# Differential attention in a list schedule: scores in halves and single PSUM banks, stacks in five transfers

## The chip, the cores and the metric

One core of one Trainium2 chip. The metric is the device time of one execution in microseconds, median of the runs; lower is better.

## What is computed

Four layers in a row, each followed by an addition and a layer normalisation of `x`, 4 x 1024 tokens of width 256: a linear attention (stage a), a gated network (stage b), a differential attention (stage c) and two blocks of local attention with a gated network (stage d). The change is in stage c:

```python
q = rope_rotate((x @ Wq.T).reshape(b, s, 2 * H, D)).reshape(b, s, H, 2, D)    # H = 8, D = 16
k = rope_rotate((x @ Wk.T).reshape(b, s, 2 * H, D)).reshape(b, s, H, 2, D)
v = (x @ Wv.T)                                          # 8 heads of 32
o1 = softmax(q1 k1^T * D ** -0.25) v
o2 = softmax(q2 k2^T * D ** -0.25) v
o = o1 - lam * o2
o = (o * rsqrt(mean(o ** 2) + EPS) * ln_w + ln_b) * (1 - LAMBDA_INIT)
return o @ Wo.T
```

There are 4 batches of 1024 tokens and 16 half heads, so 64 attention maps of 1024 x 1024.

## The kernel before

Every engine's program is written by a plan. `Plan.add` appends a step with the count of increments each engine makes in it; `play` then lets each engine emit its part of every step in the plan's order. Each engine works through its queue strictly in that order. PSUM is eight banks of 512 columns, `ps0` to `ps3` and the halves of `pw0` and `pw1`; a `Ring` hands out banks and keeps, for each, the step that frees it.

Stage c works on one map after the other, (n, sh) in the order `maps`, four maps to a group n, sixteen to a batch, in eight steps kt of 128 keys. In a step TensorE makes

- the scores of 128 keys with all 1024 queries, in two matmuls of 512 columns (lines 1327 to 1340, `half_of_s`). Their 50 rows hold q and k split into a high and a low part, and two rows with the maxima;
- beside each of them, in the other half of the array's rows, a `c_max` (line 1315), the scores of a map two places ahead (`LEAD` is 32 halves), only for their row maxima. The two are called a pair below;
- the weighting `c_w` (line 1351): exponentials times values, in two column halves at once, summed over the eight steps in one bank (the accumulator, `c_pv`).

ScalarE makes the exponential of a step's scores in one instruction of 1024 columns (line 1637) into one of two `c_p`. VectorE takes the maximum of each `c_max` (line 1922). After a map's last `c_max`, `c_mm` joins the maxima, `c_row` transposes them (TensorE, ScalarE, VectorE) and two transfers put them into `c_qst`. After a map's last weighting, ScalarE copies the accumulator out (`c_o`, line 1644), TensorE transposes it (`c_ft`, four 128x128 through line 1131) and VectorE divides. Once for four maps the normalisation follows (`c_n1` on ScalarE, `c_n2` and `c_n3` on VectorE and POOL), and per batch eight projections: `c_ot` transposes two blocks, `c_wo` multiplies (line 206).

Before a batch can start, `c_x` transposes the rows of x, `c_val` makes the values, `c_rot` the rotated q and k, `c_sum` and `c_part` on POOL split them, and `c_stack` (line 2377) copies them over SP's queue into the rows of `c_qst` and `c_kst`, once per map, in six transfers of 64 KB.

The order of stage c is written by hand in `plan_c`. `weigh()` emits the scores of step k + 1, then the weighting of step k. `finish_head`, `normalise`, `project`, `values`, `rotated` are generators that are advanced by one piece at fixed places between them. Scores take double banks (`wide`, two of them), maxima two single banks, and two banks are left: one is the accumulator, the other serves everything else in turn. Other stages use `Order`, a list scheduler: each operation has a due time, a modelled duration (`TOOK`), what it comes after, what banks it takes and gives, and the scheduler places the operation with the earliest due time among those that could start within `eps` of the first.

Of the kernel before, what the change touches and what calls it, by code (L numbers as in the profile page):

```python
# [209 lines left out]
def build(nc, A, out):  # L210
    with ExitStack() as ctx:
# [25 lines left out]
        with ExitStack() as c3:  # L237
# [295 lines left out]
        def plan_c():  # L533
            P.land("tabs", 2, "c_tabs")
            P.add("c_tabs")
            bank, sbank, wide = Ring(range(8)), Ring([]), Ring([])
# [55 lines left out]
            def weigh():
                order = [(n, sh, kt) for n, sh in maps for kt in range(8)]

                def scores(n, sh, kt):
                    P.take(wide, "c_s", n, sh, kt)
                    P.add("c_s0", n, sh, kt)
                    next(ahead, None)
                    P.add("c_s", n, sh, kt, pe=1, act=1)
                    wide.give(slot["c_s", (n, sh, kt)], ("act", "c_s", n, sh, kt))  # L600
                    if next(ahead, "end") == "end":
                        count[0] += 16

                scores(*order[0])
                for k, (n, sh, kt) in enumerate(order):
                    if k + 1 < len(order):
                        scores(*order[k + 1])
                    yield 0
                    if kt == 0:
                        slot["c_pv", (n, sh)], room["c_pv", (n, sh)] = pvb[0]  # L610
                    P.add("c_w", n, sh, kt, pe=1)
                    while late and late[0][-1] <= count[0]:
                        rows()
                    if kt == 7:
                        if n + 2 < 16:
                            held.append((n + 2, sh))
                        P.add("c_o", n, sh, act=1)
                        pvb[0] = bank.idle.pop(0)
                        bank.give(slot["c_pv", (n, sh)], ("act", "c_o", n, sh))
                        post.append(finish_head(n, sh))  # L620
                    if kt in (3, 7) and held and held[0][0] // 4 in turned_by:
                        stack(*held.pop(0))
                    yield 1

            def finish_head(n, sh):
                yield
                yield
                b, s16 = n // 4, 4 * (n % 4) + sh
                if s16 % 2:
                    P.take(bank, "c_ft", n, sh)  # L630
                    P.take(tmps, "c_odd", n, sh)
                    P.add("c_ft", n, sh, pe=1, dve=3, pool=1)
                    tmps.give(slot["c_odd", (n, sh)], ("pool", "c_ft", n, sh))
                    bank.give(slot["c_ft", (n, sh)], ("dve", "c_ft", n, sh))
                else:
                    P.use(bank, "dve", "c_ft", n, sh, pe=1, dve=2)
                if s16 % 4 == 3 and (b, s16) != (3, 15):
# [1917 lines left out]
```

## Time and profile before

| | us |
|---|---|
| median of 3 runs | 2985.62 (2983.31 to 2985.84) |
| the profiled execution | 2988.65, its span 2986.5 |
| TensorE busy in the span | 2847.9 (95%) |
| VectorE, ScalarE, POOL busy | 2170.7 (73%), 1611.5 (54%), 1049.8 (35%) |
| stage c, first score to the last c_ft | 522.7 to 1582.8 |

In the rows below, PE is TensorE, PEld its loading of weights, DVE VectorE, ACT ScalarE, SPq the queue of transfers. A timeline's row has the start, the length, the engine, the line, the operation with what it writes and reads, how many instructions are merged, and in brackets how long the engine had been idle and what ended that. A matmul's end is modelled and the next one may start before it, so costs are best read from start to start. A matmul of 32-bit values stands in two instructions, so a weighting has four.

### The profile page before, as it was taken

To read this page: it belongs to the slowest core of one execution; us is meant where nothing else is said; L and a number is where in the kernel's file an instruction comes from. 1 tells how busy PE (TensorE), PEld (TensorE's weight loads), DVE (VectorE), ACT (ScalarE), POOL (GpSimd) and SP (SyncE) were. 2 spreads that over 40 slices of the span, in tenths; PEclk is the share of its full clock that TensorE was granted. 3 is DMA by queue.
4 is the path that set the end of the run, shared out by engine and by line. 5 is a ranking of instruction groups with operands and counts; after the bars stand their busy time and mean duration, and the time that the engine had idled before them with its cause. 6 is when DMAs were issued, how large, how long until landed. Compare 5 with 4: busy or idle time off the path is not lost.

```text
span 2986.5 us, 52437 instructions
## 1 busy us (share of the span) xinstructions
PE 2847.9 (95%) x20384; PEld 1928.0 (65%) x20384; DVE 2170.7 (73%) x5057; ACT 1611.5 (54%) x2976; POOL 1049.8 (35%) x1210
## 2 busy tenths in 40 slices
PE   8998999999999999999997899999999899999997
PEld 7777877333333333333335788888888788888886
DVE  7885445777787778787865677777777577788784
ACT  3222332465555555465664566666676566666662
POOL 4333432014112211412233343444454444444441
PEclk9999999999999999999998899999999999999998
DMA  2000010220321122032202000000010100000001
GB/s 77 23 9 22 8 22 3 34 32 6 43 23 17 22 33 24 10 40 26 47 12 87 13 5 5 5 4 4 12 32 15 28 27 4 12 11 12 12 11 58
DMA packets 46795, 66.63 MB, mean 22 GB/s; under 512 B 10174, under 2 KB 34772, under 8 KB 46548
## 3 DMA queue, kind: packets, MB, share of 16 engines
q1 hardware_dynamic: 46548, 63.29, 12.0%
q8 instruction: 161, 2.64, 0.4%
q14 instruction: 86, 0.70, 0.1%
HBM read 24.99 MB, written 8.39 MB: 11 GB/s over the span
## 4 chain that ended last, share of the span: by engine, by line
PE 74%; DVE 12%; DMA 5%; ACT 3%; POOL 3%; issue 1%; SPq 1%; POOLq 0%; ACTq 0%; DVEq 0%
PE ps L1351 17%; PE pw L206 12%; PE ps L206 11%; PE pw L1327 9%; PE ps L1131 4%; DMA e_hs<-x 4%; PE pw L1131 4%; PE ps L1511 4%; PE pw L1424 2%; PE pw L1462 2%; PE pw L1281 1%; PE pw L1444 1%; PE ps L1315 1%; DVE c_mx L1922 1%; DVE stat L1791 1%
## 5 line engine op out<-in xcount | busy, mean ns | idle before, releaser
L1637 ACT ACTIVATE c_p<-pw 128x1024 f32<-128x1024 f32 x512 | 522.6, 1021 | 429.8 <-PE ps L1315 348.3
L1922 DVE TENSOR_REDUCE c_mx<-ps 128x1 f32<-128x512 f32 x1024 | 658.5, 683 | 124.4 <-PE ps L1315 120.9
L1351 PE MATMUL ps<-c_p,c_v 128*64 128x512 f32 x2048 | 555.8, 620 | 8.2 <-DVE c_mr L1935 7.7
L1315 PE MATMUL ps<-c_kst,c_qst 48*128 48x512 f32 x1024 | 386.4, 451 | 6.7 <-DMA c_kst<-shared 3.4
L1327 PE MATMUL pw<-c_qst,c_kst 50*128 50x512 f32 x1024 | 376.9, 447 | 0.8 <-DVE c_v L1895 0.8
L1327 PEld LDWEIGHTS pw<-c_qst,c_kst 50*128 50x128 f32 x1024 | 152.5, 185 | 314.9 <-issue 302.6
L1690 ACT ACTIVATE e_sm<-e_sm,e_mx 128x256 f32<-128x256 f32 x512 | 253.9, 498 | 62.6 <-DVE e_mx L2066 62.4
L2186 POOL TENSOR_SCALAR stat<-stat 128x1 f32<-128x1 f32 (+1 forms) x138 | 32.1, 233 | 669.8 <-DVE stat L1794 401.6
L206 PE MATMUL pw<-shared,e_xb 128*128 128x512 f32 x792 | 217.6, 413 | 2.3 <-DVE e_xb L2015 1.6
L2290 POOL TENSOR_TENSOR e_ss<-e_ss,half 128x16 f32<-128x16 f32 x64 | 186.7, 2918 | 87.2 <-DVE e_ss L2023 66.4
L1351 PEld LDWEIGHTS ps<-c_p,c_v 128*64 128x64 f32 x2048 | 103.0, 135 | 166.0 <-issue 128.7
L1315 PEld LDWEIGHTS ps<-c_kst,c_qst 48*128 48x128 f32 x1024 | 169.9, 185 | 28.2 <-DVE c_mx L1922 12.3
L2250 POOL TENSOR_TENSOR c_o<-c_o,c_t 128x128 f32<-128x128 f32 x32 | 14.8, 464 | 478.7 <-DVE c_t L1968 465.1
L206 PE MATMUL pw<-shared,e_w 128*124 128x512 f32 (+1 forms) x672 | 176.7, 403 | 0.4 <-ACT e_pt L1698 0.2
L1511 PE MATMUL ps<-e_w,e_hp 124*128 124x256 f32 (+1 forms) x1152 | 162.9, 291 | 8.7 <-POOL e_hp L2311 7.1
L2066 DVE CUSTOM_DVE_ANT_0 e_sm<-pw,e_mask,e_ss 128x256 f32<-128x256 f32 x354 | 152.0, 476 | 24.6 <-PE pw L1424 15.9
L1791 DVE BATCH_NORM_STATS2 stat<-x 128x6 f32<-128x256 f32 (+1 forms) x192 | 67.5, 374 | 129.6 <-DMA e_hs<-x 129.1
L206 PEld LDWEIGHTS pw<-shared,e_xb 128*128 128x128 f32 x792 | 142.2, 192 | 30.0 <-DVE e_xb L2015 1.8
L1511 PEld LDWEIGHTS ps<-e_w,e_hp 124*128 124x128 f32 (+1 forms) x1152 | 146.1, 194 | 14.6 <-POOL e_hp L2311 8.1
L206 PEld LDWEIGHTS pw<-shared,e_w 128*124 128x124 f32 (+1 forms) x672 | 120.3, 186 | 29.8 <-ACT e_of L1707 1.4
L1424 PE MATMUL pw<-e_k,e_qt 64*128 64x128 f32 x1416 | 133.1, 282 | 1.8 <-ACT e_pt L1698 0.9
L1131 PE MATMUL pw<-ident,e_sm 128*128 128x128 f32 x680 | 103.7, 280 | 22.6 <-ACT e_sm L1690 20.4
(309 smaller groups left out, 6154.7 us busy)
## 6 DMA issues: line engine op xcount, KB each, us to landing
c_qst<-shared SPq DMA_DIRECT2D x192, 64.0 KB
c_kst<-shared SPq DMA_DIRECT2D x192, 64.0 KB
x<-in_L_attn_x SPq DMA_DIRECT2D x8, 512.0 KB, 3.9
keep<-x SPq DMA_DIRECT2D x8, 512.0 KB, 4.5
e_raw<-keep SPq DMA_DIRECT2D x8, 512.0 KB, 3.5
out<-x SPq DMA_DIRECT2D x8, 512.0 KB, 5.9
e_hs<-x SPq DMA_DIRECT2D x64, 63.5 KB
e_raw<-in_L_ffn_w SPq DMA_DIRECT2D x10, 248.0 KB
```

Source lines behind the costliest of these rows:

```text
L206: ins = e.matmul(o, l, r, start=first and n == 1, stop=n == 3 * len(parts), skip_group_check=True)
L1131: ins = e.transpose(o, v, ident[0:v.shape[0], 0:v.shape[0]])
L1315: e.matmul(bank_of("c_max", n, sh, qt, h), c_qst[i][p0:p0 + 48, sh // 2, 128 * qt:128 * qt + 128], c_kst[i][p0:p0 + 48, sh // 2, 512 * h:5 ...
L1327: return e.matmul(p[:, 512 * h:512 * h + 512], c_kst[i][p0:p0 + 50, sh // 2, 128 * kt:128 * kt + 128], c_qst[i][p0:p0 + 50, sh // 2, 512 * ...
L1351: ins = e.matmul(pv[64 * h:64 * h + 64, :], c_v[b % 2][:, kt, 33 * hd:33 * hd + 64], p[:, 512 * h:512 * h + 512], start=kt == 0, stop=kt = ...
L1424: ins = e.matmul(p[r][:, c0:c0 + 128], qt[rs, hb, :], kk[rs, hb, :], start=True, stop=True, skip_group_check=True)
L1511: ins = e.matmul(o, hp[kk, l_, 128 * i:128 * i + 128], d_w2[kk, r, j, :], start=j == 0 and i % 2 == 0 and n == 0, stop=j == 5 and n == 2, ...
L1637: e.activation(c_p[kt % 2][:, :], wides[slot["c_s", (n, sh, kt)]], ACT.Exp, scale=0.5).then_inc(SC, 1)
L1690: e.activation(sm[:, q, :], sm[:, q, :], ACT.Exp, bias=mx[:, 0, q:q + 1], scale=-1.0, accum_out=mx[:, 1, q:q + 1]).then_inc(SC, 1)
L1922: e.tensor_reduce(c_mx[m % 2][:, qt, h:h + 1], bank_of("c_max", n, sh, qt, h), AX.X, ALU.max).then_inc(VE, 1)
L2066: e.tensor_tensor_reduce(d_sm[s][:, q, :], p[:, 256 * h:256 * h + 256], d_mask[:, 1 if win % 8 else 0, :], st[:, 2, head:head + 1], 3.0e38 ...
L2290: e.tensor_tensor(st[:, 1, :], st[:, 0, :], half[:, :], ALU.pow).then_inc(GP, 1)
```

## The change

Stage c is now placed by `Order`. Its operations get durations, due times (`DUE_C`, in a period `PACE` of 16.73 us per map) and their dependences; TensorE's results are held to be there 0.22 us after an operation, a change between pairs and other work to cost 0.09. With it come:

- scores are two separate operations per step, each in a single bank, of which there are three; each half has its own exponential of 512 columns (ACT `c_s`), and there are four `c_p` instead of two;
- the maxima have three banks instead of two; two banks are left for accumulator and everything else, as before, but both come from one ring;
- a stack is five transfers: one of 32 partitions and four of 16, instead of six of 16. The scratch tensor `shared` is laid out so that high and low parts lie together;
- one `c_v` (`c_vals`) instead of two, so a `c_val` waits for the weighting of the batch before that read its place;
- the weights of the next stage, its tables (`d_tabs`, with semaphores of their own) and `d_scl` are placed by the same scheduler.

```diff
+PACE, NEAR = 16.73, 0.16
+DUE_C = {"pe c_s": -2.7, "act c_s": 13.5, "dve c_max": 12.3, "dve c_mm": -8.4, "c_row": -19.7, "row_in": -24.9,
...
-                c_v = [sbin(c, f"c_v{i}", [128, 8, 296]) for i in range(2)]
-                c_p = [sbin(c, f"c_p{i}", [128, S]) for i in range(2)]
+                c_v = sbin(c, "c_vals", [128, 8, 336])
+                c_p = [sbin(c, f"c_p{i}", [128, S]) for i in range(4)]
...
-            wide.idle = [(k, tuple(a for b in (4 + 2 * k, 5 + 2 * k) for a in bank.drop(b)[1])) for k in range(2)]
-            pvb = [bank.drop(2)]
...
+            sbank.idle.append(bank.drop(4))
+            scores.idle = [bank.drop(k) for k in (5, 6, 7)]
             P.add("c_lam", dve=6, act=1)
+            order = Order(P, NEAR, {"pe": 0.22}, 0.06, 0.09)
...
+                op(at(m, "pe c_s", kt + h / 2), "pe", "c_s", i, 1, after + ([("pe", "c_s", *before)] if q else []), takes, place=place,
+                   mode="pair")
+                op(at(m, "act c_s", kt + h / 2), "act", "c_s", i, 1, [("pe", "c_s", *i)] + ([("act", "c_s", *before)] if q else []),
+                   [(weighed, "c_p", *maps[m], kt)] * (1 - h), [(scores, "c_s", *i)])
...
+                op(at(m + 1, "act c_o"), "act", "c_o", i, 1, [("pe", "c_w", *i, 7)] + ([("pe", "c_ft", *maps[m - 1])] if m else []),
+                   gives=[(bank, "c_pv", *i)])
+                op(at(m + 1, "pe c_ft"), "pe", "c_ft", i, 1, [("act", "c_o", *i)], [(bank, "c_ft", *i)])
...
+                        op(at(16 * b, "c_val", kt), "pe", "c_val", i, 1, [("dve", "c_x", b, nb, k) for k in range(2)] +
+                           [("pe", "c_w", *maps[16 * b - 1], kt)], [(bank, "c_val", *i)])
...
-            def c_s(n, sh, kt):
-                b4 = 8 * nth[n, sh] + kt
-                w.wait_ge(*pe("c_w", *maps[(b4 - 2) // 8], (b4 - 2) % 8) if b4 >= 2 else pe("c_s", n, sh, kt))
-                w.wait_ge(*pe("c_s", n, sh, kt))
-                e.activation(c_p[kt % 2][:, :], wides[slot["c_s", (n, sh, kt)]], ACT.Exp, scale=0.5).then_inc(SC, 1)
+            def c_s(n, sh, kt, h):
+                if h == 0:
+                    for s in freed("c_p", n, sh, kt):
+                        w.wait_ge(*s)
+                w.wait_ge(*pe("c_s", n, sh, kt, h))
+                e.activation(c_p[slot["c_p", (n, sh, kt)]][:, 512 * h:512 * h + 512], bank_of("c_s", n, sh, kt, h), ACT.Exp,
+                             scale=0.5).then_inc(SC, 1)
...
-                for dst, qk, order in ((c_qst[i], 0, (0, 0, 1)), (c_kst[i], 1, (0, 1, 0))):
-                    for r, part in enumerate(order):
-                        p = p0 + 16 * r
-                        e.dma_start(raw32(dst[p:p + 16, sh // 2, :]),
-                                    raw32(both[r0:r0 + 8, :, qk, part, :])).then_inc(landed, 16)
+                q, k = [raw32(both[r0:r0 + 8, qk, :, :, :]) for qk in range(2)]
+                low, high = slice(p0, p0 + 32), slice(p0 + 32, p0 + 48)
+                e.dma_start(raw32(c_qst[i][low, sh // 2, :]), q.rearrange("p m b n -> p (m b) n")).then_inc(landed, 16)
+                for b in range(2):
+                    e.dma_start(raw32(c_kst[i][p0 + b:p0 + 32:2, sh // 2, :]), k[:, :, 0, :]).then_inc(landed, 16)
+                e.dma_start(raw32(c_qst[i][high, sh // 2, :]), q[:, :, 0, :]).then_inc(landed, 16)
+                e.dma_start(raw32(c_kst[i][high, sh // 2, :]), k[:, :, 1, :]).then_inc(landed, 16)
```

How the rows move is shown at three places. L1327 before and L1381 now are scores, L1315 and L1364 maxima, L1351 and L1394 weightings, L1131 and L1180 transpositions.

TensorE in a plain map, from the first weighting of a map to the `c_ft` of the one before it; before:

```order
L1351 MATMUL ps3<-c_p0,c_v0 64x512 x2
L1327 MATMUL pw0<-c_qst1,c_kst1 128x512
L1315 MATMUL ps0<-c_kst1,c_qst1 128x512
L1327 MATMUL pw0<-c_qst1,c_kst1 128x512
L1315 MATMUL ps1<-c_kst1,c_qst1 128x512
L1351 MATMUL ps3<-c_p1,c_v0 64x512 x2
L1327 MATMUL pw1<-c_qst1,c_kst1 128x512
L1315 MATMUL ps0<-c_kst1,c_qst1 128x512
L1327 MATMUL pw1<-c_qst1,c_kst1 128x512
L1315 MATMUL ps1<-c_kst1,c_qst1 128x512
L1131 MATMUL ps2<-ident,c_pv 128x128 x4
L1351 MATMUL ps3<-c_p0,c_v0 64x512 x2
```

and now, the row of `c_p3` being the last weighting of the old map:

```order
L1381 MATMUL pw1<-c_qst1,c_kst1 128x512
L1364 MATMUL pw0<-c_kst0,c_qst0 128x512
L1394 MATMUL ps2<-c_p3,c_vals 64x512 x2
L1381 MATMUL pw0<-c_qst1,c_kst1 128x512
L1364 MATMUL ps0<-c_kst0,c_qst0 128x512
L1381 MATMUL pw1<-c_qst1,c_kst1 128x512
L1364 MATMUL ps1<-c_kst0,c_qst0 128x512
L1180 MATMUL ps3<-ident,c_pv 128x128 x4
L1394 MATMUL ps2<-c_p0,c_vals 64x512 x2
```

The `c_ft` (`c_pv`) stood behind two weightings of the new map, in the other bank; now it stands two pairs behind the last weighting of its own map and ahead of the new map's first one, which goes on in `ps2`. The scores now go through single halves. Seen from a weighting, four half scores had been issued beyond those of the steps before it, and now seven.

ScalarE at the same place (`c_pv` is `c_o`), before:

```order
L1637 ACTIVATE c_p0<-pw0 128x1024
L1613 ACTIVATE c_mr2<-ps3 8x128
L1644 ACTIVATE c_pv<-ps2 128x512
L1637 ACTIVATE c_p1<-pw1 128x1024
L1637 ACTIVATE c_p0<-pw0 128x1024
L1637 ACTIVATE c_p1<-pw1 128x1024
```

and now:

```order
L1682 ACTIVATE c_p0<-pw1 128x512
L1682 ACTIVATE c_p1<-pw0 128x512
L1682 ACTIVATE c_p1<-pw1 128x512
L1682 ACTIVATE c_p2<-pw1 128x512
L1690 ACTIVATE c_pv<-ps2 128x512
L1682 ACTIVATE c_p2<-pw0 128x512
L1682 ACTIVATE c_p3<-pw1 128x512 x2
```

What was one exponential is two, and `c_o` stands between the halves of one step.

VectorE at the start of the stage, before:

```order
L1947 TENSOR_SCALAR c_ls<-c_ls 128x1
L1922 TENSOR_REDUCE c_mx0<-ps0 128x1
L1922 TENSOR_REDUCE c_mx0<-ps1 128x1
L1922 TENSOR_REDUCE c_mx0<-ps0 128x1
L1922 TENSOR_REDUCE c_mx0<-ps1 128x1
L1935 TENSOR_TENSOR c_mr1<-ps3,c_mr1 8x128
```

and now:

```order
L1991 TENSOR_REDUCE c_ls<-c_lt 128x2
L1993 TENSOR_SCALAR c_ls<-c_ls 128x1
L1837 BN_STATS stat<-x 128x6 x4
L1840 BN_AGGR stat<-stat 128x2 x4
L1968 TENSOR_REDUCE c_mx0<-ps0 128x1
L1968 TENSOR_REDUCE c_mx0<-ps1 128x1
L1933 TENSOR_TENSOR c_xb0<-ps3,c_xb0 128x512
L1854 TENSOR_SCALAR x<-x,stat 128x256 x4
L1968 TENSOR_REDUCE c_mx0<-pw0 128x1
```

The statistics of the last tile of stage b, which came sixteen maxima later, now stand ahead of the first of them.

## Rows read from the trace of the kernel before

**Rows 1.** Busy times in stage c: length, busy us (instructions) by engine, clock, DMA, GB/s

```profile
522.70:1582.80 1060.10, 1027.68 (x4907) 387.94 (x4907) 800.93 (x1574) 590.00 (x692) 245.39 (x313) 0.99 0.22 26
```

**Rows 2.** Timeline of a plain stretch: start us, busy us, engine, line, what

```profile
1001.28 0.50 PE L1327 MATMUL pw<-c_qst,c_kst 50*128 50x512 f32 x1
...
1001.61 0.39 PE L1327 MATMUL pw<-c_qst,c_kst 50*128 50x512 f32 x1
...
1001.94 1.08 PE L1351 MATMUL ps<-c_p,c_v 128*64 128x512 f32 x4
1002.10 1.02 ACT L1637 ACTIVATE c_p<-pw 128x1024 f32<-128x1024 f32 x1 [0.65 <-PE ps L1315]
...
1002.95 0.50 PE L1327 MATMUL pw<-c_qst,c_kst 50*128 50x512 f32 x1
...
1004.63 0.27 PE L1131 MATMUL ps<-ident,c_mm 128*8 128x128 f32 x1
...
1009.07 0.66 PE L1131 MATMUL ps<-ident,c_pv 128*128 128x128 f32 x4
```

**Rows 3.** Timeline of TensorE, groups of the other kinds (two stretches)

```profile
666.69 1.67 PE L206 MATMUL ps<-c_xb,c_q 128*128 128x512 f32 x6
...
1364.88 0.44 PE L1131 MATMUL ps<-ident,c_o 128*128 128x128 f32 x2
...
1366.92 0.97 PE L206 MATMUL ps<-c_o,c_at 128*128 128x256 f32 x6
```

**Rows 4.** Busy times in five stretches, columns as in rows 1

```profile
522.70:589.68 66.98, 62.89 (x292) 25.16 (x292) 46.80 (x98) 32.70 (x40) 1.27 (x2) 0.92 0.28 32
589.68:661.75 72.07, 71.28 (x347) 24.94 (x345) 57.54 (x110) 44.56 (x51) 9.64 (x13) 1.00 0.31 34
661.75:736.39 74.64, 72.16 (x327) 28.20 (x325) 55.92 (x104) 35.89 (x41) 33.78 (x35) 1.00 0.05 6
779.69:905.67 125.98, 120.87 (x613) 49.38 (x611) 98.21 (x205) 68.54 (x84) 23.24 (x36) 1.00 0.25 28
...
1325.33:1443.28 117.95, 112.55 (x550) 42.82 (x548) 92.71 (x194) 66.01 (x80) 23.96 (x38) 0.99 0.26 28
```

**Rows 5.** Timeline of TensorE around a c_x

```profile
543.44 0.50 PE L1327 MATMUL pw<-c_qst,c_kst 50*128 50x512 f32 x1
544.27 0.49 PE L1315 MATMUL ps<-c_kst,c_qst 48*128 48x512 f32 x1 [0.34 <-DVE c_mx L1922]
...
545.30 1.08 PE L1351 MATMUL ps<-c_p,c_v 128*64 128x512 f32 x4
```

**Rows 6.** Timeline of TensorE, first weighting of a plain map after c_row

```profile
600.75 1.08 PE L1351 MATMUL ps<-c_p,c_v 128*64 128x512 f32 x4 [0.16 <-DVE c_mr L1935]
```

**Rows 7.** Timeline of TensorE at the end of the stage

```profile
1581.04 1.08 PE L1351 MATMUL ps<-c_p,c_v 128*64 128x512 f32 x4 [0.17 <-ACT c_p L1637]
1582.82 0.66 PE L1131 MATMUL ps<-ident,c_pv 128*128 128x128 f32 x4 [0.70 <-ACT c_pv L1644]
```

**Rows 8.** Groups in the stage: xcount, busy us, mean ns, idle before

```profile
L1637 ACT ACTIVATE c_p<-pw 128x1024 f32<-128x1024 f32 x512 | 522.6, 1021 | 429.8 <-PE ps L1315 348.3 <-PE pw L1327 79.0
...
L1644 ACT ACTIVATE c_pv<-ps 128x512 f32<-128x512 f32 x64 | 36.5, 570 | 1.2 <-PE ps L1351 1.2
...
L1791 DVE BATCH_NORM_STATS2 stat<-x 128x6 f32<-128x256 f32 x28 | 11.4, 415 | 0.0
```

**Rows 9.** Timeline from a batch's last c_ft to the first c_ot (two stretches)

```profile
1339.72 0.66 PE L1131 MATMUL ps<-ident,c_pv 128*128 128x128 f32 x4
...
1352.18 0.72 POOL L2274 TENSOR_TENSOR c_o<-c_o,c_lnb 128x256 f32<-128x256 f32 x1
...
1353.15 0.41 PE L1131 MATMUL ps<-ident,c_o 128*128 128x128 f32 x2 [3.11 <-POOL c_o L2274]
```

**Rows 10.** Timeline of TensorE near the start, at the lower clock

```profile
529.69 1.97 PE L1351 MATMUL ps<-c_p,c_v 128*64 128x512 f32 x4
...
532.74 1.97 PE L1351 MATMUL ps<-c_p,c_v 128*64 128x512 f32 x4
```

More of the change, by code:

```diff
@@ L44 @@
        "dve n_nm": 43.9, "d_x": -1.4}
+PACE, NEAR = 16.73, 0.16
+DUE_C = {"pe c_s": -2.7, "act c_s": 13.5, "dve c_max": 12.3, "dve c_mm": -8.4, "c_row": -19.7, "row_in": -24.9,
+         "c_stack": -4.2, "pe c_w": 4.4, "act c_o": 21, "pe c_ft": -11.4, "dve c_ft": -18.8, "pool c_ft": 27.2,
+         "c_n": -28.1, "c_val": -1, "c_x": -1.2, "c_rot": 143.7, "pool c_sum": 129.1, "pool c_part": 132.4,
+         "c_ot": 8, "c_wo": 40.4, "n_c": 19.5}
 PACE_A, NEAR_A = 8.4, 0.06
@@ L535, in plan_c @@
             P.add("c_tabs")
-            bank, sbank, wide = Ring(range(8)), Ring([]), Ring([])
+            bank, sbank, scores, weighed = Ring(range(8)), Ring([]), Ring([]), Ring(range(4))
             tmps, pairs = Ring(range(2)), Ring(range(1))
@@ L588, in rows @@
                 n, sh, _ = late.pop(0)
-                P.land(f"row{n % 2}{sh}", 2, "c_row", n, sh)
                 P.use(bank, "dve", "c_row", n, sh, pe=1, act=1, dve=1)
[L592 to L637, printed above, removed]
-                    post.append(normalise(b, s16 // 4))
-                yield
@@ L772, in plan_c, with at, moved, place @@
-            while post:
-                advance(post)
+            while late:
+                rows()
+            sbank.idle.append(bank.drop(4))
+            scores.idle = [bank.drop(k) for k in (5, 6, 7)]
+            P.add("c_lam", dve=6, act=1)
+            order = Order(P, NEAR, {"pe": 0.22}, 0.06, 0.09)
+            op = order.op
+            def at(m, key, k=0.0):
+                return PACE * (m + k / 8) + DUE_C[key]
+            def moved(due, name, count, kind, i, after):
+                def place(t):
+                    P.land(name, count, kind, *i)
+                    P.add(kind, *i)
+                    order.over_at["dma", kind, i] = t + 2.2
+                    order.settle([("dma", kind, i)])
+                op(due, "sp", kind, i, 1, after, place=place)
@@ new lines, in normalised @@
+            def normalised(b, u):
+                i, m = (b, u), 4 * (4 * b + u) + 4
+                before = [("pool", "c_n3", *divmod(4 * b + u - 2, 4))] if 4 * b + u > 1 else []
+                op(at(m, "c_n"), "act", "c_n1", i, 1, [("pool", "c_ft", 4 * b + u, sh) for sh in (1, 3)], [(tmps, "c_n1", *i)])
+                op(at(m, "c_n"), "dve", "c_n2", i, 1, [("act", "c_n1", *i)] + before, gives=[(tmps, "c_n1", *i)])
+                op(at(m, "c_n"), "pool", "c_n2", i, 2, [("dve", "c_n2", *i)])
+                op(at(m, "c_n"), "pool", "c_n3", i, 5, [("pool", "c_n2", *i)])
@@ new lines, in plan_c @@
+            i = ("b", 7)
+            op(0, "dve", "n_st", i, 8, [("dve", "b_add", 7, 1)])
+            op(0, "pool", "n_st", i, 2, [("dve", "n_st", *i)])
+            op(0, "dve", "n_nm", i, 4, [("pool", "n_st", *i)])
+            for n in range(1, 16):
+                for sh in TURN:
+                    stacked(n, sh)
+            for m in range(64):
+                for kt in range(8):
+                    for h in range(2):
+                        scored(m, kt, h)
+                weighing(m)
+                if m > 1:
+                    row(m)
@@ L774, in plan_c @@
+            for b in range(4):
+                for u in range(4 if b < 3 else 3):
+                    normalised(b, u)
+                for q in range(8 if b < 3 else 0):
+                    projected(b, q)
+                if b:
+                    rows_of(b)
+                    turned_rows(b)
+            next_layer()
+            order.run(1e8)
+            assert not order.blocked and not order.ready, (list(order.blocked)[:9], [(o["eng"], o["kind"], o["i"]) for o in order.ready])
             P.add("d_begin")
```

272 lines of the change are left out of this document (147 added, 125 removed).

## The prediction

> **What bounds the kernel now.** I read the page's busy times, then cut the trace into the stage that the change touches and into stretches of it, then timelines. The order of instructions is the same in both kernels up to the first score of the differential attention and again from the last transposition of its output, on TensorE row by row, so this stage alone is priced. It lasts 1060.1 us, from the first score at 522.70 to that transposition at 1582.80, and TensorE is busy for 1027.7 of them, VectorE for 800.9, ScalarE for 590.0 [rows 1]. So TensorE bounds it, and the question is how much of its time is waiting, open or hidden in the distance between starts.
>
> What a step costs when nothing waits is read from starts. Two score pairs and the weighting after them repeat after 1002.95 - 1001.28 = 1.67 us, of which the pairs take 0.66 and the weighting 1.01 [rows 2]. A weighting's busy time is 1.08, so a group's last matmul runs 0.07 into the next group. Less that, the c_row transposition takes 0.20 and the four of c_ft 0.59 [rows 2], the two of c_ot 0.37, c_wo 0.90, c_rot 1.60 [rows 3]. A map of eight steps is then 8 x 1.67 + 0.20 + 0.59 = 14.15 us. The whole stage: 64 x 14.15 - 0.2 (one c_row of map 1 is made before it) = 905.4, and 12 c_x (0.59), 24 c_val (0.90, the shape of c_wo), 24 c_rot, 24 c_ot, 24 c_wo: 7.1 + 21.6 + 38.4 + 8.9 + 21.6 = 97.6. Sum **1003 us**. The stage spends **57 us** above it. That is all that an order can win.
>
> Where the 57 lie [rows 4]: the first stretch lasts 66.98 against 56.3 by the counts, 10.7 lost; its clock is 0.92. Five plain maps last 72.07 against 70.75: 0.26 each, and about 27 maps are of this kind, 7 us. Four maps with eight c_rot last 74.64 against 56.6 + 12.8 = 69.4: 5.2, and there are three such stretches, 16 us. Seven maps with c_x, c_val, c_ot, c_wo last 125.98 against 118.8: 7.2, a second like it some 7.5, and the third without c_x and c_val 117.95 against 109.2: 8.7; together 23.5. The last step loses 1. Sum 58, within 1 us of the 57.
>
> **The change part by part.** *Banks of the maxima and scores.* Maxima get three banks instead of two, scores three single ones instead of two double ones. Around a c_x of the kernel before, the second maximum waits for VectorE: from 543.44 to 545.30 are 1.86 us for two pairs that need 0.66 [rows 5]. One more bank lets VectorE be later by half a step or more before TensorE stops. VectorE is busy 57.54 of 72.07 us in plain maps and 98.21 of 125.98 in the fullest ones [rows 4], so it can catch up. This is the largest gain, in the 33 maps with extra work. Bounds for what these maps lose now, 39 us: nothing of it goes, or all.
>
> *Place of the accumulator.* Before, a new map's weighting takes the bank that c_row has just used, and waits 0.16 for the DVE c_mr that empties it [rows 6]; this, with what it shifts, is the 0.26 of a plain map. In the new order c_row has its own bank, and the new map goes on in the bank that c_o empties, or in the other.
>
> *The new wait.* Before, c_ft stands behind two weightings of the next map, over 3 us after the last weighting. Now only two pairs lie between: the order gives c_ft 1.01 + 0.66 = 1.67 us. The kernel before has this case once, at its end, with ScalarE idle: the last weighting starts at 1581.04, c_ft at 1582.82, 1.78 us [rows 7]. So at least 0.11 is lost per map, 7 us over 63 maps, if the ACT c_o finds its engine free. It stands behind the exponentials of the pairs before that weighting. An exponential of half the width is not in the trace: 1.021 us for 1024 columns bounds it above, half of it, 0.51, below, and the nearest row is c_o itself, 512 columns at 0.570 [rows 8]; I take 0.59. An exponential starts 0.49 after its pair (1002.10 after 1001.61) [rows 2]. For pairs 0.66 and 0.33 ahead of the weighting that is -0.17 and, behind the first, +0.42, so the second ends 1.01 after the weighting's start, and the weighting's last matmul ends at 1.08 [rows 2]. They just fit. I take 0.11 and keep 0.68 (one exponential more ahead) for the range. What is queued behind c_o on ScalarE are exponentials with 2.5 steps of lead: the weighting now stands seven half scores behind instead of four, with four c_p. Behind c_ft on TensorE stand the new map's first weighting and all the rest.
>
> *ScalarE by halves:* 512 x (2 x 0.59 - 1.02) = 82 us more, 672 of some 1030: hidden under TensorE, and without the seven halves of lead it would cost 0.16 per step at most.
>
> *Stacks, SP and POOL.* Five transfers instead of six carry the same bytes. A stack must be there for maxima two maps ahead of its scores, six maps after the score that frees its place: nothing gained, nothing lost. The row transfers stand behind one stack per map at worst and have a map of slack. On POOL the d_scl and the six weight splits swap places; both are before the last three head groups. Two c_fill fewer: nothing, they run beside c_val. One c_v instead of two ties c_val to the last weightings of the batch before: pairs and a weighting (1.34 us or more) lie between two c_val, against 0.42 us of copy.
>
> *Moved work near POOL.* The first c_ot of a batch follows c_ft of its last map through DVE, POOL and ACT. Before, that took from 1339.72 to 1353.15, 13.4 us, once with 3.1 us of stall [rows 9]. In the new order 5 weightings, 4 c_val and 9 pairs lie between, 0.59 + 5.05 + 3.6 + 2.97 = 12.2: about 1 us lost in each of three batches, 3 us in all. A c_rot pair on one bank with one weighting and one pair between (five times) leaves 1.34 us to two DVE operations of 0.69 and those ahead of them: 0.3 to 1.0 each, 3 us.
>
> *The start.* The eight statistics of the last b tile now stand ahead of the first maxima: four at 0.415 [rows 8] and four shorter ones, 2 to 4 us on VectorE, where the second step waited for a maximum anyway. Three banks give half of it back. I leave the 10.7 at 10, keeping 7 and 14.
>
> **Sum.** Start 10 + plain maps 27 x 0.11 = 3 + c_rot maps 12 x 0.11 + 3 = 4.3 + the 21 fullest maps 21 x 0.11 + 3 for c_ot + 4 for queued VectorE work = 9.3 + end 1 = 27.6 us above 1003, against 57: **29 us less**. The profiled execution took 2988.65 (span 2986.5 and 2.1 around it) and would take 2959; the median of the runs is 3.0 lower, 2985.62, so I predict **2957 us**, 1.0% faster. A measurement of this kernel tells 0.2%, 6 us, from no change.
>
> **The rivals.** *VectorE keeps the full maps* (0.14): its queue, not the banks, is late there, 39 us stay and only the plain maps and part of the rot maps gain: about 11 us, **2975**. For it: VectorE's share rises to 78%, and in-order waits as for c_mr remain. Against: its idle time there is over 20%.
>
> *The clock flickers* (0.05). In the first stretch TensorE waited and then ran at half clock: a weighting and the pairs ahead of the next one took 532.74 - 529.69 = 3.05 us instead of 1.67 [rows 10], at 1.2 and not 2.4 GHz. If the new short stops at every map did this for a twentieth of the stage, 51 us at 3.05 instead of 1.67 lose 23: **2980**. Against it: five plain maps with a stop each have a clock of 1.00 [rows 4]. The Trainium skill (TensorE: Matmul & The Clock Gate, A second HAM failure mode: psum-queue depth-cycling) says that frequent short idles between groups of matmuls, as banks are cycled, can make the clock swing between its levels. By that rule the change is mostly eaten; by the row on plain maps it is not, and I side with the row.
>
> *The order does not do what it says* (0.07): it rests on durations (a step of 1.78 by its table, 1.67 in the trace) and every engine's queue is strict, so new waits appear where the plan sees none, and 57 stay 57 within 6: **2986**.
>
> *c_o comes late: slower* (0.08). If one more exponential is ahead of c_o or halves take 0.7 and more, c_ft starts 0.11 + 0.57 = 0.68 late in each of 63 maps: 43 us in place of 7. Then 27.6 + 36 = 64 against 57: **2993**. It decides from (57 - 20.6) / 63 = 0.58 us per map, where the gain is gone. For it: nothing but two pairs covers c_o, once per map. Against: ScalarE has more than a quarter of its time free.
>
> **How the numbers follow.** Forecast 0.66, from 2944 (20 us more of the full maps' and start's waits gone, less what c_o takes) to 2970. The range goes on to the VectorE case and stops short of the others: **2943 to 2979**, leaving out 0.2. Faster: forecast and VectorE case, 0.80. Same: the order case and part of the clock's, 0.11. Slower 0.09.
>
> **What would show it.** Right: the stage lasts about 1031 us; plain maps take 14.2 to 14.3 from c_ft to c_ft; c_ft's wait for c_pv is 0.1 in each; hardly any maximum waits for VectorE; ACT busy near 670. Wrong: plain maps over 14.4 (c_o late), clock below 0.95 in the middle of the stage, or maxima still waiting in the maps with c_val and c_wo; or a score that waits for a row's transfer.

## The result and the profile after

The changed kernel takes **2959.48 us** (median of 4 runs, 2956.85 to 2962.04) against 2985.73 (4 runs, 2983.31 to 2988.52): a ratio of 0.9912, 95% interval 0.9895 to 0.9929. Forecast were 2957 us, between 2943 and 2979. The profiled execution took 2961.68 us, its span 2959.4.

Busy times by stretch: the stage, the plain maps 4 to 7, the maps 8 to 11 with rotations, maps 16 to 23 and 48 to 55 with c_val and projections, and all that follows the stage. Columns as in [rows 1].

```profile
520.89:1552.20 1031.31, 1014.23 (x4911) 367.15 (x4910) 806.38 (x1575) 632.89 (x1204) 244.58 (x313) 1.00 0.22 27
591.00:648.08 57.08, 56.94 (x278) 17.91 (x277) 46.05 (x88) 38.27 (x74) 8.78 (x11) 1.00 0.27 29
648.08:717.64 69.56, 69.42 (x325) 26.29 (x324) 56.35 (x104) 38.39 (x74) 33.44 (x35) 1.00 0.02 3
780.77:911.75 130.98, 129.82 (x663) 49.35 (x661) 108.43 (x220) 82.98 (x160) 22.41 (x34) 1.00 0.23 25
1312.42:1440.52 128.10, 127.22 (x647) 47.70 (x645) 105.67 (x216) 81.02 (x156) 22.38 (x34) 1.00 0.23 25
1552.20:2957.00 1404.80, 1322.28 (x11107) 1140.72 (x11105) 1035.66 (x2738) 869.32 (x2000) 601.97 (x638) 0.97 0.06 19
```

The stage lasts 1031.3 us instead of 1060.1 [rows 1], 28.8 less; the span shrank by 27.1 (1.8 less ahead of the stage, 3.5 more behind it). A plain map takes 57.08 / 4 = 14.27 us. Four rotation maps take 69.56 against 69.4 by the prediction's counts, where it was 5.2 above them before [rows 4]. Maps 16 to 23 hold eight steps each and five c_val, eight c_ot, seven c_wo, four c_x: 113.2 + 4.5 + 3.0 + 6.3 + 2.3 = 129.3, measured 130.98; before, seven such maps lost 7.2.

The groups that answer to [rows 8], in the stage (count, busy us, mean ns, idle before):

```profile
L1682 ACT ACTIVATE c_p<-pw 128x512 f32<-128x512 f32 x1024 | 562.3, 595 | 341.2 <-PE ps L1364 183.5 <-PE pw L1364 87.8 <-PE pw L1381 46.5
...
L1690 ACT ACTIVATE c_pv<-ps 128x512 f32<-128x512 f32 x64 | 38.2, 598 | 13.7 <-PE ps L1394 13.7
...
L1837 DVE BATCH_NORM_STATS2 stat<-x 128x6 f32<-128x256 f32 x28 | 11.7, 426 | 0.8
```

TensorE around the c_ft that opens map 5 (the last weighting of map 4 starts at 602.90), and the stage's end, which answers to [rows 7]:

```profile
602.90 1.08 PE L1394 MATMUL ps<-c_p,c_vals 128*64 128x512 f32 x4
...
604.68 0.66 PE L1180 MATMUL ps<-ident,c_pv 128*128 128x128 f32 x4
605.26 1.08 PE L1394 MATMUL ps<-c_p,c_vals 128*64 128x512 f32 x4
...
1551.79 0.65 PE L1180 MATMUL ps<-ident,c_pv 128*128 128x128 f32 x4 [0.70 <-ACT c_pv L1690]
```

From weighting to c_ft are 1.78 us where 1.67 is work: the 0.11 of the forecast. The waits of TensorE in the stage show what it did not have:

```profile
PE pw L1381 <- DMA c_qst<-c_mr: 9.0, 8, 2.4
...
PE ps L1394 <- ACT c_p L1682: 1.4, 1, 1.4
```

Eight times a score waits for its map's row (the transfer of c_mr into c_qst), 9.0 us in all. No wait on a maximum stands among the longer ones, and none on POOL before the stage's end. With each map's length from its first weighting to the next map's, less the counts, 28 us above 1003 are left (good to about 1 us a line, as a c_wo that stands at the border of two maps can be given to either):

| maps | above the counts, before | after | forecast |
|---|---|---|---|
| 0 to 3, and what stands ahead | 11.0 | 8.8 | 10 |
| a plain map | 0.26 | 0.11 | 0.11 |
| 12 rotation maps | 16 | 0.4 | 4.3 |
| 26 other maps with c_val or projections | 23.5 | 2.7 | 9.3 |
| 13 to 15, 29 to 31, 45 to 47 | 2.3 | 14.7 | in the plain maps |

The forecast's sum held; two of its terms did not. One that it set at nothing holds about 16 us: 4.2 us in map 1, and most of the last line. Two that it kept, the waits of the maps with extra work and those of the start, are for the most part gone.

### The profile page after: what moved, and what is told of

Same layout as the page of the kernel before. It is cut to its first block, busy times and chain, and to the rows that moved or that the text cites. A ratio compares the mean times of both kernels' runs of the same rounds, so it can differ in the third digit from the quotient of the medians.

```text
span 2959.4 us, 52471 instructions
## 1 busy us (share of the span) xinstructions
PE 2835.6 (96%) x20384; PEld 1908.3 (64%) x20384; DVE 2176.4 (74%) x5057; ACT 1653.3 (56%) x3488; POOL 1048.7 (35%) x1208
## 4 chain that ended last, share of the span: by engine, by line
PE 75%; DVE 11%; DMA 6%; POOL 3%; ACT 2%; issue 1%; SPq 1%; POOLq 0%; DVEq 0%; ACTq 0%
PE ps L1394 17%; PE pw L218 13%; PE ps L218 11%; PE pw L1381 10%; PE ps L1180 5%; DMA e_hs<-x 4%; PE pw L1180 4%; PE ps L1554 4%; PE pw L1467 2%; PE pw L1505 2%; PE pw L1330 1%; PE pw L1487 1%; DVE stat L1837 1%; DVE e_ot L2132 1%; PE ps L1467 1%
## 5 line engine op out<-in xcount | busy, mean ns | idle before, releaser
L1682 ACT ACTIVATE c_p<-pw 128x512 f32<-128x512 f32 x1024 | 562.3, 595 | 341.2 <-PE ps L1364 183.5
L1394 PE MATMUL ps<-c_p,c_vals 128*64 128x512 f32 x2048 | 547.4, 618 | 2.7 <-ACT c_p L1682 1.4
L1968 DVE TENSOR_REDUCE c_mx<-ps 128x1 f32<-128x512 f32 x694 | 462.7, 683 | 114.3 <-PE ps L1364 106.7
L1381 PE MATMUL pw<-c_qst,c_kst 50*128 50x512 f32 x1024 | 385.1, 449 | 9.4 <-DMA c_qst<-c_mr 9.0
L1381 PEld LDWEIGHTS pw<-c_qst,c_kst 50*128 50x128 f32 x1024 | 154.5, 185 | 368.2 <-ACT c_p L1682 272.1
L1364 PE MATMUL ps<-c_kst,c_qst 48*128 48x512 f32 x694 | 289.5, 452 | 4.6 <-DMA c_kst<-shared 3.5
L1968 DVE TENSOR_REDUCE c_mx<-pw 128x1 f32<-128x512 f32 x330 | 225.5, 683 | 47.3 <-PE pw L1364 43.8
L1394 PEld LDWEIGHTS ps<-c_p,c_vals 128*64 128x64 f32 x2048 | 104.2, 135 | 181.2 <-issue 162.1
L1364 PE MATMUL pw<-c_kst,c_qst 48*128 48x512 f32 x330 | 148.2, 449 | 0.0
```

The costliest lines, as they stand in the source:

```text
L1364: e.matmul(bank_of("c_max", n, sh, qt, h), c_qst[i][p0:p0 + 48, sh // 2, 128 * qt:128 * qt + 128], c_kst[i][p0:p0 + 48, sh // 2, 512 * h:5 ...
L1381: e.matmul(bank_of("c_s", n, sh, kt, h), c_kst[i][p0:p0 + 50, sh // 2, 128 * kt:128 * kt + 128], c_qst[i][p0:p0 + 50, sh // 2, 512 * h:512 ...
L1394: ins = e.matmul(pv[64 * h:64 * h + 64, :], c_v[:, kt, 33 * hd:33 * hd + 64], p[:, 512 * h:512 * h + 512], start=kt == 0, stop=kt == 7, sk ...
L1682: e.activation(c_p[slot["c_p", (n, sh, kt)]][:, 512 * h:512 * h + 512], bank_of("c_s", n, sh, kt, h), ACT.Exp, scale=0.5).then_inc(SC, 1)
L1968: e.tensor_reduce(c_mx[m % 2][:, qt, h:h + 1], bank_of("c_max", n, sh, qt, h), AX.X, ALU.max).then_inc(VE, 1)
```

## The experiments

All are edits of the changed kernel unless it says otherwise. Ratios are to the kernel before, on the same chip; the changed kernel stands at 0.9912.

### Fewer stacks per map

SP's queue around the end of the first batch, in the changed kernel: start, length, transfer.

```profile
716.28 0.72 SPq L2438 DMA_DIRECT2D c_qst<-shared  x1
...
722.27 1.29 SPq L2438 DMA_DIRECT2D c_qst<-shared  x1
...
729.85 1.27 SPq L2438 DMA_DIRECT2D c_qst<-shared  x1
...
736.75 2.23 SPq L2451 DMA_DIRECT2D c_qst<-c_mr  x2
739.02 0.71 SPq L2438 DMA_DIRECT2D c_qst<-shared  x1
...
744.69 1.26 SPq L2438 DMA_DIRECT2D c_qst<-shared  x1
...
752.00 2.53 SPq L2451 DMA_DIRECT2D c_qst<-c_mr  x2
```

The first stack of a pair takes 5.7 us (739.02 to 744.69), the second 7.3 (to 752.00), the row 2.5: 15.5 us or more for a map of 14.27. The queue falls behind, and the row is last in it. TensorE, at the row of 752.00 (the first line is the c_row that the row waits for):

```profile
741.84 0.27 PE L1180 MATMUL ps<-ident,c_mm 128*8 128x128 f32 x1
...
754.44 0.50 PE L1364 MATMUL pw<-c_kst,c_qst 48*128 48x512 f32 x1
756.08 0.50 PE L1381 MATMUL pw<-c_qst,c_kst 50*128 50x512 f32 x1 [1.14 <-DMA c_qst<-c_mr]
```

So the row sets out 10.2 us behind its c_row, lands at 754.5, and the score that TensorE was ready for at 754.94 waits. The length of a pair and a row is not the whole of it, since it was as long before the change and no score waited. SP's queue and the c_row of the kernel before:

```profile
748.81 2.18 SPq L2393 DMA_DIRECT2D c_qst<-shared  x3
...
761.82 2.53 SPq L2403 DMA_DIRECT2D c_qst<-c_mr  x2
764.39 2.19 SPq L2393 DMA_DIRECT2D c_qst<-shared  x3
```

```profile
760.84 0.27 PE L1131 MATMUL ps<-ident,c_mm 128*8 128x128 f32 x1
```

A pair and a row took 15.6 us there too, but the pair set out right behind a row, and the next row left 1.0 us behind its c_row. In the changed kernel three stacks in a row (716.28 to 736.75) had gone ahead of the first of these rows, whose c_row stood at 727.17, and the pairs behind it left no room to catch up.

The edit, **e_spread**, holds a stack back until a given map has been scored:

```diff
                 after = [("pe", "c_s", n - 2, sh, 7, 1)] if n > 1 else []
+                b, j = divmod(nth[n, sh], 16)
+                from_ = 16 * b + (-4, -3, -2, -1, 0, 1, 1, 2, 2, 3, 4, 4, 5, 6, 7, 8)[j]
+                if from_ > 0:
+                    after.append(("pe", "c_s", *maps[from_ - 1], 7, 1))
```

> The plan may issue a stack's five transfers no earlier than a table says, so that two stacks seldom fall into one map and a row's transfer stands behind one stack. Theory A (the row transfers of maps 2, 13 to 15, 29 to 31 and 45 to 47 come late because SP's queue takes 7.4 + 7.4 + 2.4 us, more than a map's 14.3 us): the scores' waits on c_qst<-c_mr, 9.0 us in all, and most of what maps 1, 13 to 15, 29 to 31 and 45 to 47 take over 14.15 us go; 8 to 15 us less than the changed kernel, about 2948 us. Rival 1 (those maps are long for the rotations and c_val anyway): the waits on c_mr go and others take their place, 2957 to 2961 us. Rival 2 (the stacks themselves come too late when held back): waits on the stacks' transfers (c_kst, c_qst<-shared) of some us each, slower than 2962.

Measured: **2944.68 us, ratio 0.9852 (0.9838 to 0.9865)**. Its waits in the stage begin with

```profile
PE ps L1398 <- ACT c_p L1686: 1.9, 2, 1.5
PE ps L218 <- DVE c_at L2048: 0.8, 3, 0.3
```

and the row transfer is gone from them. The stage lasts 1015.4 us, 15.9 less; maps 13 and 14 take 14.27 each instead of 14.67 and 15.76, map 47 takes 17.26 instead of 22.17. Theory A holds, at the top of its range or a little above it (14.8 us by the medians, 15.9 by the stage). More went (15.9) than the waits added up to (9.0), for the most part because of the clock: map 47 lost 4.9 us with a stop of 1.70, map 1 lost 4.2 with one of 2.36, together 5.0 more than they waited. The stretch of map 47 in the changed kernel, with a stop of 1.70 us in it, and of map 14's end and map 15 with one of 1.14, then map 47 without a stop in e_spread:

```profile
1290.25:1312.42 22.17, 20.47 (x89) 8.62 (x88) 13.26 (x27) 9.50 (x18) 3.88 (x8) 0.85 0.40 62
756.08:771.36 15.28, 14.57 (x69) 4.61 (x69) 11.34 (x21) 9.55 (x18) 0.87 (x2) 1.00 0.44 50
```

```profile
1279.37:1296.63 17.26, 17.19 (x88) 6.90 (x88) 12.96 (x27) 9.39 (x18) 0.87 (x2) 1.00 0.31 33
```

After the stop of 1.70 us a weighting takes 1.98 us, the half clock of [rows 10]:

```profile
1300.14 0.50 PE L1381 MATMUL pw<-c_qst,c_kst 50*128 50x512 f32 x1 [1.70 <-DMA c_qst<-c_mr]
...
1300.64 1.08 PE L1394 MATMUL ps<-c_p,c_vals 128*64 128x512 f32 x4
...
1304.58 1.98 PE L1394 MATMUL ps<-c_p,c_vals 128*64 128x512 f32 x4
```

After the stop of 1.14 the clock stayed at 1.00. But the length of the stop alone does not decide this. In **e_ft** below, a stop of 1.33 us was followed by a stretch at a mean clock of 0.72, and one of 1.73 by a stretch at 1.00. The two stops, and the stretches behind them:

```profile
1013.24 0.49 PE L1381 MATMUL pw<-c_qst,c_kst 50*128 50x512 f32 x1 [1.73 <-DMA c_qst<-c_mr]
...
1283.79 0.49 PE L1381 MATMUL pw<-c_qst,c_kst 50*128 50x512 f32 x1 [1.33 <-DMA c_qst<-c_mr]
```

```profile
1013.50:1027.00 13.50, 13.50 (x67) 4.17 (x65) 10.07 (x19) 8.76 (x17) 0.00 (x0) 1.00 0.49 55
1284.00:1290.00 6.00, 6.00 (x23) 1.61 (x22) 3.00 (x6) 2.73 (x6) 0.00 (x0) 0.72 0.48 50
```

### One number of the plan

**e_pace** changes a duration that the scheduler reckons with, and nothing else:

```diff
-        "dve c_row": 0.27, "sp row_in": 2.5, "sp c_stack": 5.9, "pe c_w": 0.92, "act c_o": 0.56, "pe c_ft": 0.46,
+        "dve c_row": 0.27, "sp row_in": 2.5, "sp c_stack": 7.4, "pe c_w": 0.92, "act c_o": 0.56, "pe c_ft": 0.46,
```

> One number of the changed kernel's plan: a stack is reckoned at 7.4 us (what the second of a pair takes) instead of 5.9. On SP's queue the row of map 14, of 30 and of 46 then stands in front of a pair of stacks instead of behind it; TensorE's order changes in one place, the order of VectorE and ScalarE nowhere. Theory A (rows behind stacks, and the half clock that follows a long stop, hold 15 us): the waits of maps 13, 29 and 45 go, those of 14, 15, 30, 31, 46 and 47 shrink by what the queue was ahead, the waits on c_qst<-c_mr fall from 9.0 to 3 to 7 us, and the time by 3 to 10 us, to 2950 to 2957. Rival (the queue has the same work in those 45 us, so the last row comes as late): within 3 us of the changed kernel.

Measured: **2943.20 us, ratio 0.9860 (0.9844 to 0.9877)**, 15 us less than the changed kernel. On SP's queue a row went ahead of a pair not at three places but at four: map 2's too, at the stage's start, and that alone gave 4.2 us (map 1 takes 15.48 us instead of 19.68). Map 14:

```profile
732.66 2.25 SPq L2451 DMA_DIRECT2D c_qst<-c_mr  x2
734.95 0.71 SPq L2438 DMA_DIRECT2D c_qst<-shared  x1
...
740.62 2.55 SPq L2451 DMA_DIRECT2D c_qst<-c_mr  x2
```

Maps 14, 30 and 46 are back at 14.27, map 47 at 17.47. Only maps 13, 29 and 45 keep 0.3 to 0.5 us. I had expected 3 to 10 us. The queue has the same work, but with one row put ahead of a pair each time, the rows that follow leave 2.8 to 5.6 us behind their c_row and no longer 10, which is within their slack, and the half clock goes with the stops. So the loss is an order on one queue, from a duration that was short by 1.5 us.

### Six transfers or five

**e_six** puts the six transfers of 16 partitions back into the changed kernel; **e_five** puts the five into the kernel before (with `shared` laid out as they need). Their core, from e_six:

```diff
-                e.dma_start(raw32(c_qst[i][low, sh // 2, :]), q.rearrange("p m b n -> p (m b) n")).then_inc(landed, 16)
...
+                for dst, qk, order in ((c_qst[i], 0, (0, 0, 1)), (c_kst[i], 1, (0, 1, 0))):
+                    for r, part in enumerate(order):
```

> The changed kernel with six-transfer stacks of 16 partitions each, in the same order. Theory 1 (SP's queue takes about 1.25 us for a transfer behind another, whatever its size): a stack takes 1.2 us longer, a pair 2.4, the rows behind pairs come later and the waits on c_qst<-c_mr (9.0 us) at least double: 2968 to 2985 us. Theory 2 (a stack's time goes by its bytes and partitions; in the kernel before six transfers took 5.7 to 7.1 us, about as long as five now): within 4 us of the changed kernel, waits on c_mr 5 to 12 us.

> The kernel before with the change's five-transfer stacks (and the layout of shared that they need), nothing else. The prediction's term for this part is 0: no row waits for a stack there, and the pair of six-transfer stacks at 748.81 to 761.8 us (13.0 us) is no slower than a pair of five-transfer ones after the change (722.27 to 736.75, with one more ahead: 14.5 us): within 3 us of the kernel before. Rival (the queue was the bound): 5 us or more faster.

Measured: e_six 2956.55 us, 0.9903 (0.9887 to 0.9920), its waits on rows 5.4 us in 7 places; e_five 2986.59 us, 0.9999 (0.9989 to 1.0008). Neither differs from its base. e_six's queue shows why (two stacks and a row):

```profile
736.16 2.18 SPq L2439 DMA_DIRECT2D c_qst<-shared  x3
...
741.83 4.43 SPq L2439 DMA_DIRECT2D c_qst<-shared  x3
...
748.81 2.57 SPq L2449 DMA_DIRECT2D c_qst<-c_mr  x2
```

The pair takes 736.16 to 748.81 = 12.7 us with twelve transfers; in the changed kernel 739.02 to 752.00 = 13.0 with ten. Theory 1, a price per transfer whatever its size, falls.

### Two banks for the maxima

**e_max2** takes the third bank away; **e_max2s** does the same with the stacks spread.

```diff
-            sbank.idle.append(bank.drop(4))
+            bank.drop(4)
```

> The changed kernel with two banks for the maxima's scores instead of three; the plan is made anew for two. Theory of the prediction (the third bank is the largest part of the gain, since VectorE's other work of the rotation and projection maps then fits between): the waits on maxima come back in the rotation and projection maps, up to the 16 + 23.5 us that they held before, at least half of it: 2975 to 2995 us; plain maps stay at 14.27. Rival (the list schedule's order alone removed them): within 4 us of 2959.

> Stacks spread as in e_spread, and two banks for the maxima's scores instead of three. In e_max2 plain maps took 14.68 us instead of 14.27 and maps with other work 0.1 to 0.4 more, but three stops (maps 12 and 13, 28 and 29, 44 and 45) with the half clock behind them took 10, 6 and 4 us, and those stand behind row transfers. Theory A (the third bank is worth 0.4 us in a plain map and little elsewhere; the long stops were the rows' alone): the stage takes 16 to 20 us more than in e_spread, no stop above 2 us, ratio to before about 0.991. Rival (the third bank hides stops of other kinds too): 25 us or more.

Measured: e_max2 2980.38 us, 0.9974 (0.9965 to 0.9984); e_max2s 2959.87 us, 0.9909 (0.9895 to 0.9924). The first hit its range for a wrong reason: plain maps did not stay at 14.27, and long stops on rows lay beside them. The second has no stop on a row. One plain map and maps 17 to 23, in e_max2s and then in e_spread:

```profile
606.06:620.74 14.68, 14.64 (x71) 5.09 (x70) 11.31 (x23) 9.45 (x18) 0.00 (x0) 1.00 0.26 28
804.07:914.10 110.03, 109.52 (x549) 44.14 (x549) 91.98 (x187) 70.04 (x137) 14.54 (x25) 1.00 0.29 32
```

```profile
602.11:616.37 14.26, 14.23 (x70) 4.46 (x69) 11.25 (x22) 9.43 (x19) 0.00 (x0) 1.00 0.27 30
796.95:905.72 108.77, 108.26 (x549) 39.66 (x550) 91.92 (x187) 70.30 (x137) 14.51 (x25) 1.00 0.29 32
```

The third bank is worth 0.42 us in a plain map and 1.26 / 7 = 0.18 in a map with projections; maps 16 to 23 together take 132.26 us with two banks (781.84 to 914.10), 0.4 a map above the counts of 129.3, where such maps lost 7.2 / 7 = 1.0 before the change and lose 0.2 with three. So it is not the third bank, but the rest of the change, that cleared most of the full maps. Which part of it, the order as such, the scores in halves that let it be so fine, or the four c_p, these runs do not separate.

### c_ft one weighting later

**e_ft** takes up the 0.11 us: c_ft of a map is planned behind the next map's first weighting. **e_both** adds it to e_spread.

```diff
-                op(at(m + 1, "pe c_ft"), "pe", "c_ft", i, 1, [("act", "c_o", *i)], [(bank, "c_ft", *i)])
+                op(at(m + 1, "pe c_ft"), "pe", "c_ft", i, 1, [("act", "c_o", *i)] + ([("pe", "c_w", *maps[m + 1], 0)] if m < 63 else []), [(bank, "c_ft", *i)])
```

> The transposes of c_pv (c_ft) are planned behind the next map's first weighting instead of ahead of it. Theory (of the prediction: in a plain map 0.11 us of TensorE's time is the wait for the copy of c_pv): plain maps take 14.15 us instead of 14.27, 63 x 0.11 = 7 us less, about 2952 us. Rival (the copy then holds the bank longer, or the stop moves to the weighting): plain maps stay at 14.25 or more, 2957 to 2962 us.

> Both edits: the stacks spread over the maps and c_ft behind the next map's first weighting. If both theories hold and the two gains lie in different maps, they add: 15 to 22 us less than the changed kernel, about 2941 us. If the waits on rows only hide the others, less than the larger of the two alone plus 3 us.

Measured: e_ft **2981.37 us, 0.9981 (0.9972 to 0.9990)**, e_both 2964.38 us, 0.9919 (0.9905 to 0.9932): each 20 us slower than its base. The theory holds where it spoke, plain maps take 14.17 us. The maps with other work pay for it. There the new plan has c_ft, a projection and a new accumulator in the same two banks, which may be the reason, though no run tests it; these maps take 0.2 to 0.4 us more each, maps 24 and 40 1.7, and map 57 has a stop of 2.47 us with the low clock behind it. In e_both, the stop, and map 57, which takes 20.00 us where its steps and one c_wo give 14.15 + 0.90 = 15.05:

```profile
1453.48 0.50 PE L1368 MATMUL ps<-c_kst,c_qst 48*128 48x512 f32 x1 [2.47 <-DVE c_mx L1972]
```

```profile
1454.51:1474.51 20.00, 20.00 (x77) 7.06 (x76) 13.26 (x27) 8.77 (x18) 7.76 (x10) 0.74 0.14 40
```

**e_plain** keeps the edit at 27 places (the expectation says 28), nearly all in maps without other work (`if m + 1 in {1, 4, 5, 6, 7, 8, 12, ...}`) and spreads the stacks.

> Stacks spread over the maps (as in e_spread), and c_ft behind the first weighting only where a map holds no other work (28 of 63). In e_ft and e_both the maps without other work took 14.17 us instead of 14.27, those with rotations, transposes or projections 0.2 to 0.4 longer, and two had stops of 1.7 and one of 8 us. If that is the whole account: 28 x 0.10 = 2.8 us less than e_spread, a ratio to the kernel before of about 0.984. If the plan made anew brings a long stop elsewhere: more than e_spread.

Measured: **2940.04 us (2939.94 to 2940.20), ratio 0.9843 (0.9829 to 0.9858)**, the best version, ahead of both kernels. Against e_spread's 0.9852 the intervals overlap; its stage is 4.3 us shorter (1011.2 to 1015.4), where 2.8 was expected. About 1.3 of it lies at the start and is not the edit's, as far as can be seen: there e_spread's profiled run fell to a clock of 0.82 (520.60 to 530.00) and e_plain's did not.

```profile
521.91:1533.07 1011.16, 1004.99 (x4908) 363.09 (x4907) 804.72 (x1575) 631.18 (x1204) 244.80 (x313) 1.00 0.23 27
601.19:615.37 14.18, 14.18 (x72) 4.47 (x70) 11.27 (x22) 9.44 (x20) 0.00 (x0) 1.00 0.27 30
```

### The price of a late c_o

**e_late** prices the fourth rival. Two dependences are added:

```diff
-                op(at(m + 1, "act c_o"), "act", "c_o", i, 1, [("pe", "c_w", *i, 7)] + ([("pe", "c_ft", *maps[m - 1])] if m else []),
+                op(at(m + 1, "act c_o"), "act", "c_o", i, 1, [("pe", "c_w", *i, 7)] + ([("act", "c_s", *maps[m + 1], 3, 0)] if m < 63 else []) + ([("pe", "c_ft", *maps[m - 1])] if m else []),
...
-                       [("act", "c_s", *i, kt, 1), ("dve", "c_val", b, kt // 4, kt % 4)] + [before] * (m + kt > 0),
+                       [("act", "c_s", *i, kt, 1), ("dve", "c_val", b, kt // 4, kt % 4)] + [before] * (m + kt > 0) + [("pe", "c_ft", *maps[m - 1])] * (m > 0 and kt == 0),
```

> The changed kernel with each copy of c_pv held back on ScalarE behind one more exponential, and c_ft kept in front of the next map's first weighting. It prices the prediction's fourth rival (0.68 us a map, decided where the copy stands on ScalarE). By that mechanism: each of 63 maps 0.6 to 0.95 us longer with the wait at c_ft, 38 to 60 us, 2997 to 3020. Rival (the scores and weightings that are planned around it cover it): under 10 us.

Measured: 3004.64 us, 1.0065 (1.0044 to 1.0086), 46 us more than the changed kernel. A plain map, and map 14, with its wait for a row:

```profile
606.81:621.62 14.81, 14.59 (x70) 5.28 (x69) 11.15 (x22) 9.33 (x18) 0.00 (x0) 1.00 0.25 29
752.50:776.66 24.16, 17.59 (x70) 5.92 (x70) 11.34 (x22) 9.44 (x18) 0.00 (x0) 0.79 0.38 44
```

```profile
765.43 0.79 PE L1381 MATMUL pw<-c_qst,c_kst 50*128 50x512 f32 x1 [6.36 <-DMA c_qst<-c_mr]
```

14.81 - 14.27 = 0.54 us a map, 34 us over 63; the rest is in maps 14 and 30, where rows come later still. The size is near the rival's (0.57 more a map), but the wait is not where the rival has it. The plan, made anew, draws four more pairs ahead of c_ft (six where there were two), and scores wait for exponentials, 62 times, 14.3 us in all:

```profile
619.29 0.49 PE L1381 MATMUL pw<-c_qst,c_kst 50*128 50x512 f32 x1 [0.22 <-ACT c_p L1682]
...
621.04 0.66 PE L1180 MATMUL ps<-ident,c_pv 128*128 128x128 f32 x4
```

So a late copy costs about half a microsecond a map even in a plan that makes room for it, and the changed kernel does not run into it. What it costs with the order left as it is, no run shows.

## Why the prediction was right, point by point

- *What bounds the stage, and its floor.* 1003 us by counts. e_plain's stage lasts 1011.2, within 8 us of this floor. It is soft by a few us: single maps with a projection came out up to 0.2 us under their counts.
- *The new wait.* 0.11 us at each c_ft, as taken from [rows 7]; e_ft and e_plain remove it and get 14.17. The copy found ScalarE free, as the two exponentials ahead of it ended sooner than reckoned. The exponential by halves was taken at 0.59 and is 0.595. c_o is 0.598 where [rows 8] has 0.570.
- *ScalarE by halves, "672 us".* 632.9. Two exponentials side by side take 1.09 us together, not 1.19, as the second starts before the first has ended; the cost was hidden either way.
- *Banks of the maxima, "the largest gain, in the 33 maps with extra work".* Half wrong. The waits there went, more fully than forecast (3 us left of 39, where 13.6 were expected). But the third bank is not what did most of it: e_max2s keeps most of that gain without it. What in the rest of the change did it stays open. The third bank pays in the plain maps, where the new order, denser in maxima, would lose 0.5 us without it.
- *The chain through POOL, 3 us, and c_rot pairs, 3 us.* Neither shows: rotation maps are on their counts, no c_ot waits for POOL. The plan put enough between them, which I had counted at exactly the edge.
- *Stacks: "nothing gained, nothing lost".* Right for five instead of six (e_five, e_six).
- *"The row transfers stand behind one stack per map at worst and have a map of slack."* **This step failed.** Where the next batch's parts become ready, and at the start, two or three stacks stand ahead of a row. A pair and a row take 15.5 us of a 14.27 us map, and rows left about 10 us behind their c_row. The slack was about what the prediction said: a row was wanted 13.1 us after its c_row (741.84 to 754.94). What was wrong is the one stack. It cost 15.9 us (e_spread), and 15 come back with one duration (e_pace). The rows of SP's queue before the change already showed a stack at 5.7 to 7.1 us; I did not add two and a row up against a map. It stood in the text only as what would make it wrong.
- *The start, 10.* 8.8, but 4.2 of it is map 1's wait for a row with the half clock after it; the part I had in mind is 4.6.
- *The clock.* TensorE: Matmul & The Clock Gate of the Trainium skill (A second HAM failure mode: psum-queue depth-cycling) would have had short stops between groups make the clock swing. This case does not agree: in the changed kernel the plain maps have a stop of 0.11 each and a clock of 1.00. The half clock followed single longer stops, in the changed kernel those of 2.36 and 1.70 us, and those I had not priced: 15.9 us for 9.0 us of waits.

So that the total was met is luck. A loss of 16 us not seen stood against 15 us of waits that I had kept and that went: 10.5 in rotation and full maps, and some 5 at the start. Without the rows' loss the stage is 12.4 us above its floor (e_spread), not the 27.6 of the forecast.

## What to carry to other kernels

Where a scheduler decides the order, check the durations it reckons with on every queue against the trace, under load: a stack behind another took 7.3 us, not 5.9, and that one number was worth 15 us. Add up what one period puts on each queue, and put what is small and due first in front of what is large and has slack. Judge an edit to such a plan by all kinds of stretches: c_ft one weighting later gained its 0.1 us in every plain map and lost 20 us over the kernel.

## What the runs showed of the hardware

- On SP's queue a stack's first transfer (32 partitions) took 0.71 us in most places where no other stack stood right ahead of it, and 1.25 to 1.3 behind a stack; the others took 1.25 to 1.8; a row of two transfers takes 1.34 us alone and 2.5 behind a stack. Ten transfers of a pair took 13.0 us and twelve with the same bytes 12.7.
- A stop of TensorE of 1.14 us left the clock at 1.00; with stops of 1.70 (map 47), 2.47 (map 57 of e_both) and 6.36 us (map 14 of e_late) go stretches with a mean clock of 0.85, 0.74 and 0.79. In e_ft a stop of 1.33 us was followed by 0.72 over the next 6 us, and one of 1.73 by 1.00, so the length alone does not tell. Such a stop costs more than itself: 4.9 us for the 1.70, 9.4 for the 6.36 (24.16 against 14.81 of a plain map of e_late).
- Two exponentials of 512 columns, 0.595 us each, took 1.08 to 1.09 us together; one of 1024 columns took 1.02.
